# First block of a graph-attention layer: four whole products of 65 weight columns in place of tiles of columns

## The chip, the cores and the metric

The kernel runs on one NeuronCore of a Trainium2 chip. The metric is the device time of one execution in microseconds (us). TensorE (PE in the profile) multiplies, VectorE is DVE, ScalarE is ACT, GpSimd is POOL, SyncE is SP. TensorE's clock has two levels here, 1.2 GHz (granted clock 0.50) and 2.4 GHz (1.00).

## The reference, cut to what matters

A graph of 3125 nodes and 53125 edges goes through a layer norm, two graph-attention layers (four heads of 64 channels, then one of 256), a second norm and a mixture of eight experts, two per node. The change sits in the first attention layer:

```
h = (x @ W1).reshape(n, 4, 64)
es = (h * a_src).sum(-1);  ed = (h * a_dst).sum(-1)
e = leaky_relu(es[src] + ed[dst], 0.2)
w = exp(e - segment_max(e, dst)[dst])
den = segment_sum(w, dst)
out = segment_sum(h[src] * (w / den[dst])[:, :, None], dst)
```

For each destination node and head the kernel needs a sum of 64 values over its sources and one sum of weights (`den`), 65 numbers in all.

## The kernel before, in words

Nodes lie in 25 tiles of 128. `c[s, d]` counts the edges from source s to destination d. For most destinations the layer is computed densely: a matrix of weights, source by destination, is built for each head and multiplied by a table `slots` which holds, for each source and head, 64 values and one column of row factors.

Layer 1 takes its destinations in five blocks (`B1`): block 0 is one tile (128 columns), blocks 1 to 4 are three tiles (384 columns). A block has 25 **steps**, one per source tile; the step's number over all blocks is q, so block 0 is q = 0 to 24. In a step, in this order of dependence:

- ACT (L1062, four instructions, one per head) writes the ratios into one of three buffers `S1` (in `ring_a`). For buffer q it waits until TensorE has finished step q - 3.
- DVE (L1958) multiplies them by the counts in `arena`. In block 0 it then scales the table tile s + 2 (`scale`, L1848), and it builds the one-hot rows for the next step's visits (L1696, and L1700 three times).
- PE makes three **passes** (L1350). Pass 0 computes the values of heads 0 and 1 as two tiles of 64 columns of the array side by side, into the two halves of bank 0. Pass 1 does heads 2 and 3 in bank 1. Pass 2 computes the four weight sums as four tiles of 32 columns in bank 2, from one column that is repeated 32 times. So a step has eight matmuls in fp32, and each of them shows as two MATMUL records in the trace.
- Ahead of each pass PE makes one **visit** (L1198), a bf16 matmul over the whole array that counts edges for a later block: three visits, of 400, 275 and 175 columns, make one **window** of 16 destinations in one bank. ACT copies a finished window into `arena` (`window_out`, L910), after it has written `S1` of the step two later. The windows take turns in banks 3, 4 and 5 (`BANK_AT`); only the first 8 use two banks, 4 and 5.

After a block's last step ACT copies the sums to `spare` (`sums_out`, L1017), and PE must wait for each copy (semaphore `s_ot`) before it writes that bank in the next block. Then PE turns the sums so that nodes lie on partitions (L1312, L1314; "spread").

Destinations that are not in a dense block are reached edge by edge, in pairs of windows: POOL gathers their table rows (L830) once SP has stored all 25 scaled tiles (L726). Each pair is multiplied in a given step, the first in q = 28 (`PAIR1`), and its weights are made by DVE one step ahead.

The order on each engine is written out by hand as loops over q; nothing reorders it.

Of the kernel before, what the change touches and what calls it, by code (L numbers as in the profile page):

```python
# [5 lines left out]
P = 128  # L6
# [21 lines left out]
VISITS = 3  # L28
# [108 lines left out]
    USES += [("window", w) for w, v, u in VISITS_AT.get(_q, ()) if v == 0]  # L137
    USES += [("pair", p) for p in PAIR1_AT.get(_q, ())]
USE_OF = {_use: _n for _n, _use in enumerate(USES)}
N_EARLY = B1[0][1] * PER_TILE  # L140
BANK_AT = [4 + n % 2 if n < N_EARLY else 3 + n % 3 for n in range(len(USES))]
USE_BEFORE = [max((m for m in range(n) if BANK_AT[m] == BANK_AT[n]), default=None) for n in range(len(USES))]

# [104 lines left out]
def build(nc, x, src, dst, g_w1, g_a1s, g_a1d, g_b1, g_lng, g_lnb, g_w2, g_a2s, g_a2d, g_b2,  # L248
# [19 lines left out]
    with ExitStack() as ctx:  # L268
# [157 lines left out]
        vT = F2[0:NT * HEADS, 0:P]  # L426
        Wg = ring_a[:, 0:NT * P].rearrange("p (s n) -> p s n", s=NT)
        OT = spare[:, 0:PASSES * 384].rearrange("p (h n) -> p h n", h=PASSES)
        Ct = spare[:, 0:1600].bitcast(u16).rearrange("p (s n) -> p s n", s=NT)
        gd_f, glo_f, ghi_f, gkk_f = (spare[:, k * GCOLS:(k + 1) * GCOLS] for k in range(4))  # L430
        wbase = spare[:, 4 * GCOLS:4 * GCOLS + WCOLS]
# [461 lines left out]
        def _(act):  # L893
# [118 lines left out]
            def sums_out(b):  # L1012
                n = B1[b][1] * P
                after(act, s_tr, B1[b][0])
                for i in range(PASSES):
                    act.wait_ge(s_mm, ((b + 1) * NT - 1) * PASSES + i + 1)
                    act.activation(OT[:, i, 0:n], bank[i][:, 0:n], ACT.Copy).then_inc(s_ot, 1)  # L1017

# [155 lines left out]
        def _(pe):  # L1174
# [128 lines left out]
            def hooks1(q):  # L1303
                for g, i, t in tiles_at(G1, spread_of, q):
                    pe.wait_ge(s_ot, (block_of(t) + 1) * PASSES)
                    after(pe, s_TS, NT + TURNS_BEFORE["spread", t])
                    after(pe, s_xb, SPREADS_BEFORE["spread", t])
                    if t == 0:
                        pe.wait_ge(s_lk, 2)
                    by_head = bank[6][:, 0:W1T].rearrange("p (h c) -> p h c", c=CH + 1)  # L1310
                    for k in range(HEADS // 2):
                        pe.matmul(by_head[:, 2 * k:2 * k + 2, 0:CH], OT[:, k, i * P:(i + 1) * P],  # L1312
                                  ident[:, :].rearrange("p (h c) -> p h c", h=2), start=True, stop=True)
                    pe.matmul(by_head[:, :, CH], OT[:, HEADS // 2, i * P:(i + 1) * P], ident[:, 0:P:PW], start=True, stop=True).then_inc(s_tr, 1)  # L1314
                for g, i, t in tiles_at(G1, turn_of, q):
                    pe.wait_ge(s_xn, NT + E1[t] + 1)
                    pe.wait_ge(s_TS, NT + TURNS_BEFORE["turn", t])
                    after(pe, s_xb, SPREADS_BEFORE["turn", t])
                    for k in range(2):
                        ins = pe.transpose(bank[6][:, k * P:(k + 1) * P], xn[:, E1[t] % 4, k * P:(k + 1) * P], ident[:, :])  # L1320
                    ins.then_inc(s_T, 1)
                for g, i, t in tiles_at(G1, turn_of, q, 3):
                    e = E1[t]
                    pe.wait_ge(s_TS, NT + e + 1)
                    pe.wait_ge(s_HS, NT + e)
                    pe.wait_ge(s_HE, NT + e)
                    for k in range(2):
                        ins = pe.matmul(bank[7][:, 0:D + 2], xnT[:, e % 4, k, :], w2a[:, k, :], start=(k == 0), stop=(k == 1))
                    ins.then_inc(s_H, 1)

            q = 0
            for b, (t0, kt) in enumerate(B1):
                w_ = kt * P
                for s in range(NT):
# [4 lines left out]
                    for i in range(PASSES):  # L1339
# [4 lines left out]
                        if s == 0 and b:  # L1344
                            pe.wait_ge(s_ot, (b - 1) * PASSES + i + 1)
                        values = i < HEADS // 2
                        for h in range(2 * i, 2 * i + 2) if values else range(HEADS):
                            to = bank[i][h % 2 * CH:(h % 2 + 1) * CH, 0:w_] if values else bank[i][h * PW:(h + 1) * PW, 0:w_]
                            weights = row[:, h, 0:CH] if values else row[:, h, CH:CH + 1].broadcast_to([P, PW])
                            ins = pe.matmul(to, weights, S1[q % SLOTS1][:, h * w_:(h + 1) * w_], start=(s == 0), stop=(s == NT - 1))  # L1350
# [839 lines left out]
```

## Time and profile before

| | |
|---|---|
| median of 3 runs | 1428.64 us |
| the three runs | 1430.99, 1428.64, 1409.08 us |
| the profiled execution | 1437.54 us |
| span of its trace | 1435.5 us |
| mean granted clock of TensorE | 0.896 |
| TensorE matmul busy | 1216.6 us, 85% of the span |
| DVE busy | 853.8 us, 59% |
| ACT busy | 702.5 us, 49% |
| POOL busy | 711.8 us, 50% |

Busy shares are means over stages that have different limits. The slices of the page show where TensorE is busy and which clock it had; the chain of waits shows which engine sets the end; the timeline shows one step, instruction by instruction. A start in the timeline is more exact than a duration, since matmuls overlap and their ends are modelled: the price of a piece of work in a row of such pieces is read from one start to the next.

### The profile page before, as it was taken

The page shows a single profiled execution, that of the slowest core. Times are in us where ns is not written, and L with a number is a line of the kernel's source. Part 1 is how long each engine was busy: PE and PEld are TensorE (multiplying, and loading weights), DVE is VectorE, ACT ScalarE, POOL GpSimd, SP SyncE. Part 2 cuts the span into 40 slices and gives each one's busy share as a digit, 9 for nine tenths or more (in the row PEclk, how much of TensorE's full clock was granted, in tenths as well). Part 3 has the DMA queues.
Part 4 walks back from the last instruction along what each step waited for, and adds up shares of the span by engine and source line. Part 5 has one row for each costly group of instructions (what it writes and reads, how often), then busy time and mean ns, then how long its engine had stood idle before and what let it go on. Part 6 is the DMA issues. An engine that isn't in the chain of part 4 may idle for free.

```text
span 1435.5 us, 26517 instructions
## 1 busy us (share of the span) xinstructions
PE 1216.6 (85%) x8723; PEld 800.5 (56%) x8724; DVE 853.8 (59%) x2522; ACT 702.5 (49%) x1854; POOL 711.8 (50%) x621
## 2 busy tenths in 40 slices
PE   3789888888888988957787787794699999999997
PEld 3533333333333333335464565563699999999996
DVE  8677788888789979733565765786422222222221
ACT  3656566757577767833343343341434344334432
POOL 1000677676668874026665666640144445454544
PEclk9955798899999999968788899897799999999999
DMA  5232643643564382063544554544033332323221
GB/s 162 86 95 73 150 110 104 175 122 94 148 152 108 101 213 71 27 232 94 157 140 152 163 182 125 164 110 115 12 94 93 95 97 37 95 37 97 35 37 26
DMA packets 137158, 157.16 MB, mean 109 GB/s; under 512 B 58935, under 2 KB 116504, under 8 KB 137064
## 3 DMA queue, kind: packets, MB, share of 16 engines
q0 software_dynamic: 33616, 73.02, 21.5%
q1 hardware_dynamic: 102888, 82.42, 18.7%
q8 instruction: 52, 0.85, 0.2%
q10 hardware_dynamic: 560, 0.52, 0.1%
q14 instruction: 42, 0.34, 0.1%
HBM read 121.19 MB, written 35.52 MB: 109 GB/s over the span
## 4 chain that ended last, share of the span: by engine, by line
PE 50%; DVE 22%; issue 11%; ACT 5%; another core or an unknown queue 5%; DMA 4%; POOL 2%; DVEq 0%; POOLq 0%; SPq 0%; ACTq 0%
PE bank L1480 11%; PE bank L1488 11%; PE bank L1350 10%; PE bank L1431 6%; DVE ring_a L1958 4%; PE bank L1198 3%; ACT ring_a L1062 2%; DVE ohk L1700 2%; POOL arena L830 2%; DVE ring_a L2018 2%; DMA out_x<-ring_a,si 2%; PE bank L1401 1%; DVE st L1553 1%; DVE ohs L1696 1%
## 5 line engine op out<-in xcount | busy, mean ns | idle before, releaser
L830 POOL DMA_INDIRECT arena<-rows,idx_e x365 | 411.9, 1128 | 334.0 <-issue 90.6
L1350 PE MATMUL bank<-ring_a,slots 128*64 128x384 f32 (+1 forms) x2000 | 331.1, 518 | 44.6 <-DVE ring_a L1958 34.5
L1431 PE MATMUL bank<-h2t,ring_a 128*128 128x257 f32 x700 | 194.0, 423 | 29.5 <-DVE ring_a L2018 15.6
L1958 DVE SCALAR_TENSOR_TENSOR ring_a<-ring_a,arena 128x1536 f32<-128x1536 f32 (+1 forms) x125 | 192.6, 1541 | 41.9 <-ACT ring_a L1062 28.7
L1062 ACT ACTIVATE ring_a<-vbb,slots 128x384 f32<-128x384 f32 x400 | 212.2, 605 | 7.2 <-DMA vbb<-v_rows 4.1
L1170 ACT ACTIVATE ring_a<-bank,cols 128x128 f32<-128x128 f32 x432 | 129.0, 371 | 160.9 <-PE bank L1480 160.6
L1431 PEld LDWEIGHTS bank<-h2t,ring_a 128*128 128x128 f32 x700 | 141.4, 212 | 66.2 <-issue 29.1
L1350 PEld LDWEIGHTS bank<-ring_a,slots 128*64 128x64 f32 x2000 | 81.5, 136 | 133.0 <-issue 64.4
L876 POOL DMA_INDIRECT gs<-gates,gk x54 | 51.4, 951 | 149.3 <-DVE gk L2110 136.0
L1480 PEld LDWEIGHTS bank<-ring_a,arena 128*128 128x128 f32 x1056 | 123.1, 192 | 1.7
L1480 PE MATMUL bank<-ring_a,arena 128*128 128x128 f32 x1056 | 123.2, 275 | 0.0
L1488 PE MATMUL bank<-arena,ring_a 128*128 128x256 f32 x528 | 119.4, 379 | 0.0
L1198 PE MATMUL bank<-ohk,ohs 128*128 128x400 bf16 x336 | 112.1, 340 | 7.9 <-DVE ohk L1700 3.7
L830 POOL DMA_INDIRECT vbb<-rows,idx_e x75 | 98.2, 1309 | 36.1 <-issue 17.7
L2018 DVE SCALAR_TENSOR_TENSOR ring_a<-ring_a,p,arena 128x256 f32<-128x256 f32 x175 | 79.4, 480 | 58.3 <-ACT ring_a L1141 46.4
L2106 DVE TENSOR_SCALAR ring_a<-bank,cols 128x128 f32<-128x128 f32 x110 | 40.1, 406 | 118.8 <-PE bank L1463 111.8
L1141 ACT ACTIVATE ring_a<-vbb,np,pu 128x256 f32<-128x256 f32 x175 | 95.9, 590 | 28.7 <-remote 24.2
L865 POOL DMA_INDIRECT ring_a<-xtab,gi x55 | 54.3, 988 | 108.6 <-DVE gi L2098 98.3
L1488 PEld LDWEIGHTS bank<-arena,ring_a 128*128 128x128 f32 x528 | 97.7, 190 | 11.9
L870 POOL DMA_INDIRECT out_x<-ring_a,si x55 | 89.6, 1628 | 21.1 <-issue 16.3
L2114 DVE TENSOR_TENSOR ring_a<-bank,vbb 128x256 f32<-128x256 f32 x54 | 22.9, 425 | 125.3 <-PE bank L1488 119.0
L1198 PEld LDWEIGHTS bank<-ohk,ohs 128*128 128x128 bf16 x336 | 33.8, 101 | 112.0 <-issue 66.6
(308 smaller groups left out, 1709.4 us busy)
## 6 DMA issues: line engine op xcount, KB each, us to landing
counts_all<-arena SPq DMA_DIRECT2D x14, 800.0 KB
arena<-counts_all SPq DMA_DIRECT2D x14, 800.0 KB
arena<-in_L_ffn_W SPq DMA_DIRECT2D x8, 1024.0 KB, 7.4
vbb<-v_pairs SPq DMA_DIRECT2D x23, 320.0 KB
arena<-rows,idx_e POOLq DMA_INDIRECT x365
XB<-general_sums SPq DMA_DIRECT2D x38, 130.0 KB
vbb<-in_L_ffn_W SPq DMA_DIRECT2D x4, 1024.0 KB
spare<-in_L_ffn_W SPq DMA_DIRECT2D x4, 1024.0 KB
```

The costliest lines, as they stand in the source:

```text
L830: pool.indirect_dma_start(to[:, k, 0:width], None, table, bass.IndirectOffsetOnAxis(idx_e[:, m * PAIR + k:m * PAIR + k + 1], 0)).then_inc( ...
L870: pool.indirect_dma_start(out, bass.IndirectOffsetOnAxis(si[:, 0:1], 0), ys, None, bounds_check=N - 1, oob_is_err=False, compute_op=ALU.ad ...
L1062: ins = act.activation(S1[q % SLOTS1][:, h * k * P:(h + 1) * k * P].rearrange("p (t n) -> p t n", n=P), (vb1 if b else vb0)[:, 0:k, h, :], ...
L1141: act.activation(S2[m % SLOTS2][:, 0:k * P], vb2[j % 2][:, 0:k * P], ACT.Relu, scale=pu2[:, s, 0:1], bias=np2[:, s, 0:1]).then_inc(s_r, 1)
L1170: act.activation(hid[:, f, :], bank[HB[f // 2]][:, (f % 2) * P:(f % 2 + 1) * P], ACT.Gelu, bias=cols[:, ds(e * FC + f, 1)]).then_inc(s_hg, 1)
L1198: pe.matmul(bank_of(("window", w))[:, 0:KEYS].rearrange("p (h d) -> p h d", d=WIN)[:, :, lo:hi], ohs[:, w % 4, v, :], ohk[:, u % 8, 0:NT * ...
L1350: ins = pe.matmul(to, weights, S1[q % SLOTS1][:, h * w_:(h + 1) * w_], start=(s == 0), stop=(s == NT - 1))
L1431: ins = pe.matmul(bank[(j % 2) * 2 + i][:, 0:W2T], S2[q2 % SLOTS2][:, i * P:(i + 1) * P], h2t[:, s, 0:W2T], start=(s == 0), stop=(s == NT ...
L1480: ins = pe.matmul(bank[HB[f // 2]][:, (f % 2) * P:(f % 2 + 1) * P], fw1[c][:, k, f * P:(f + 1) * P], xeT[:, k, :], start=(k == 0), stop=(k ...
L1488: ins = pe.matmul(bank[3][:, 0:D], hid[:, f, :], fw2[c][:, f, :], start=(f == 0), stop=(f == FC - 1))
L1958: v.scalar_tensor_tensor(a, a, 1.0, C1[b][:, s, 0:k * P].unsqueeze(1).broadcast_to([P, HEADS, k * P]), ALU.max, ALU.mult).then_inc(s_a, 1)
L2018: v.scalar_tensor_tensor(a, a, p2[:, s, 0:1], C2[j % 2][:, 0:k, s, :], ALU.add, ALU.mult).then_inc(s_a, 1)
```

## The change

In block 0 alone PE makes, for each head, one matmul with all 65 columns of the head's table row (64 values and the factor) as weights, into partitions 0 to 64 of a bank of its own: heads 0 to 3 in banks 0 to 3. Pass 0 holds head 0, pass 1 head 1, pass 2 heads 2 and 3. Eight matmuls a step become four. Blocks 1 to 4 stay as they were.

What follows from it: bank 3 is no longer free for windows in q = 0 to 25, so `N_EARLY` grows and these windows take turns in banks 4 and 5. `sums_out(0)` copies four pieces of 65 partitions instead of three of 128. The spread of tile 0 is four transposes instead of three matmuls.

```diff
-N_EARLY = B1[0][1] * PER_TILE
+N_EARLY = N_FIRST // VISITS + len({w for q in range(NT + 1) for w, v, u in VISITS_AT.get(q, ()) if v == 0})
+assert PAIR1[0] > NT
 BANK_AT = [4 + n % 2 if n < N_EARLY else 3 + n % 3 for n in range(len(USES))]
...
+        OT0 = spare[0:CH + 1, 0:HEADS * P]
...
             def sums_out(b):
-                for i in range(PASSES):
+                for h in range(HEADS) if b == 0 else ():
+                    act.wait_ge(s_mm, (NT - 1) * PASSES + min(h + 1, PASSES))
+                    ins = act.activation(OT0[:, h * P:(h + 1) * P], bank[h][0:CH + 1, 0:P], ACT.Copy)
+                    if h != PASSES - 1:
+                        ins.then_inc(s_ot, 1)
+                for i in range(PASSES) if b else ():
...
+                    if t == 0:
+                        for h in range(HEADS):
+                            ins = pe.transpose(bank[6][:, h * (CH + 1):(h + 1) * (CH + 1)], OT0[:, h * P:(h + 1) * P], ident[0:CH + 1, 0:CH + 1])
+                        ins.then_inc(s_tr, 1)
+                        continue
...
-                        for h in range(2 * i, 2 * i + 2) if values else range(HEADS):
+                        for h in range(i, HEADS if i == PASSES - 1 else i + 1) if b == 0 else ():
+                            ins = pe.matmul(bank[h][0:CH + 1, 0:P], slots[:, s, h * (CH + 1):(h + 1) * (CH + 1)],
+                                            S1[q % SLOTS1][:, h * P:(h + 1) * P], start=(s == 0), stop=(s == NT - 1))
+                        for h in () if b == 0 else range(2 * i, 2 * i + 2) if values else range(HEADS):
```

PE in steps q = 0 and 1, before. The visits are the rows with `ohk,ohs` (25x11 is 275 columns, 25x7 is 175), the passes are those with `ring_a,slots` (weight columns x moving columns):

```order
L1198 MATMUL bank5<-ohk,ohs 128x400
L1350 MATMUL bank0<-ring_a,slots 64x128 x2
L1198 MATMUL bank5<-ohk,ohs 128x25x11
L1350 MATMUL bank1<-ring_a,slots 64x128 x2
L1198 MATMUL bank5<-ohk,ohs 128x25x7
L1350 MATMUL bank2<-ring_a,slots 32x128 x4
L1198 MATMUL bank3<-ohk,ohs 128x400
L1350 MATMUL bank0<-ring_a,slots 64x128 x2
```

The same place now:

```order
L1205 MATMUL bank4<-ohk,ohs 128x400
L1360 MATMUL bank0<-ring_a,slots 65x128
L1205 MATMUL bank4<-ohk,ohs 128x25x11
L1360 MATMUL bank1<-ring_a,slots 65x128
L1205 MATMUL bank4<-ohk,ohs 128x25x7
L1360 MATMUL bank2<-ring_a,slots 65x128
L1360 MATMUL bank3<-ring_a,slots 65x128
L1205 MATMUL bank5<-ohk,ohs 128x400
```

Every matmul of a step now takes 65 or 128 weight columns, where full-width and tiled ones alternated, and the windows no longer use bank 3.

ACT from the last window of block 0 to the copies of its sums (q = 25 and 26), before:

```order
L1062 ACTIVATE ring_a<-vbb,slots 128x384 [waits step_summed,v_rows_loaded]
L1062 ACTIVATE ring_a<-vbb,slots 128x384 x3
L910 ACTIVATE arena<-bank4 128x25x16 [waits visits_summed]
L1062 ACTIVATE ring_a<-vbb,slots 128x384 [waits step_summed]
L1062 ACTIVATE ring_a<-vbb,slots 128x384 x3
L1017 ACTIVATE spare<-bank0 128x128 [waits step_summed]
L1017 ACTIVATE spare<-bank1 128x128 [waits step_summed]
L1017 ACTIVATE spare<-bank2 128x128 [waits step_summed]
```

The same place now:

```order
L1069 ACTIVATE ring_a<-vbb,slots 128x384 [waits step_summed,v_rows_loaded]
L1069 ACTIVATE ring_a<-vbb,slots 128x384 x3
L912 ACTIVATE arena<-bank5 128x25x16 [waits visits_summed]
L1069 ACTIVATE ring_a<-vbb,slots 128x384 [waits step_summed]
L1069 ACTIVATE ring_a<-vbb,slots 128x384 x3
L1019 ACTIVATE spare<-bank0 65x128 [waits step_summed]
L1019 ACTIVATE spare<-bank1 65x128 [waits step_summed]
L1019 ACTIVATE spare<-bank2 65x128 [waits step_summed]
L1019 ACTIVATE spare<-bank3 65x128 [waits step_summed]
```

There is one copy more, at the same place.

## Rows read from the trace of the kernel before

**Rows 1.** The page: TensorE's busy tenths and clock in 40 slices.

```profile
PE   3789888888888988957787787794699999999997
...
PEclk9955798899999999968788899897799999999999
```

**Rows 2.** The chain of waits from 76 to 150 us, shares by line.

```profile
by line: PE bank L1350 61.5%; PE bank L1198 34.8%; PE bank L1207 1.7%; DVE ring_a L1958 0.9%; DVE slots L1848 0.9%; DVE arena L1954 0.3%; issue 0.2%; DVEq L1955 0.0%
```

**Rows 3.** Stretches: us, length, PE busy (last row PE, PEld, DVE, ACT, POOL), clock, DMA.

```profile
67.30:70.70 3.40, 1.04 (x6) 1.00 0.02 5
...
152.60:156.00 3.40, 3.26 (x10) 0.50 1.01 234
156.00:159.40 3.40, 2.73 (x18) 1.00 1.24 291
363.00:380.00 17.00, 16.73 (x175) 1.00 0.45 121
...
77.50:150.30 72.80, 72.76 (x482) 28.61 (x482) 53.10 (x148) 44.52 (x122) 7.12 (x7) 0.50 0.29 91
```

**Rows 4.** Timeline of TensorE in q = 1 (start us, us, engine, line, operation).

```profile
80.02 0.52 PE L1198 MATMUL bank<-ohk,ohs 128*128 128x400 bf16 x1
...
80.46 0.70 PE L1350 MATMUL bank<-ring_a,slots 128*64 128x128 f32 x4
...
81.09 0.43 PE L1198 MATMUL bank<-ohk,ohs 128*128 128x275 bf16 x1
...
81.45 0.69 PE L1350 MATMUL bank<-ring_a,slots 128*64 128x128 f32 x4
...
82.08 0.35 PE L1198 MATMUL bank<-ohk,ohs 128*128 128x175 bf16 x1
...
82.35 0.66 PE L1350 MATMUL bank<-ring_a,slots 128*32 128x128 f32 x8
...
82.94 0.52 PE L1198 MATMUL bank<-ohk,ohs 128*128 128x400 bf16 x1
```

**Rows 5.** Full-width and lone 64-column matmuls, weight loads (min/median/max ns), and clock.

```profile
70.63 2.06 PE L1267 MATMUL bank<-ident,v 128*128 128x128 f32 x8 [1.47 <-ACT v L963]
...
1060.90 1.84 PE L1480 MATMUL bank<-ring_a,arena 128*128 128x128 f32 x15
...
L1480 PEld LDWEIGHTS bank<-ring_a,arena x1056: 190/192/192, 1045.8 to 1422.3; 128*128 128x128 f32 x176
...
1009.62 12.63 PE L1454 MATMUL bank<-h2t,arena 128*64 128x128 f32 x100 [8.70 <-ACT arena L1157]
...
1009.30:1012.70 3.40, 3.08 (x15) 0.50 0.00 0
1012.70:1016.10 3.40, 3.40 (x33) 0.99 0.00 0
```

**Rows 6.** Timeline of DVE: its multiply in q = 1 and in q = 4.

```profile
78.82 0.68 DVE L1958 SCALAR_TENSOR_TENSOR ring_a<-ring_a,arena 128x512 f32<-128x512 f32 x1
...
84.88 0.68 DVE L1958 SCALAR_TENSOR_TENSOR ring_a<-ring_a,arena 128x512 f32<-128x512 f32 x1
```

**Rows 7.** Timeline of ACT in one step of block 0.

```profile
82.46 0.50 ACT L910 ACTIVATE arena<-bank 128x400 uint16<-128x400 f32 x1 [1.03 <-PE bank L1198]
83.08 1.28 ACT L1062 ACTIVATE ring_a<-vb,slots 128x128 f32<-128x128 f32 x4
```

**Rows 8.** Timeline at the end of block 0 (PE and ACT).

```profile
147.71 0.35 PE L1198 MATMUL bank<-ohk,ohs 128*128 128x175 bf16 x1
...
151.77 0.28 ACT L1017 ACTIVATE spare<-bank 128x128 f32<-128x128 f32 x1 [0.76 <-PE bank L1350]
...
152.19 1.55 PE L1350 MATMUL bank<-ring_a,slots 128*64 128x384 f32 x4 [1.46 <-ACT spare L1017]
```

**Rows 9.** POOL's first gather, and SP's stores of the 25 scaled tiles.

```profile
141.36 1.44 POOL L830 DMA_INDIRECT arena<-rows,idx_e  x1 [65.95 <-DMA rows<-slots]
...
81.81 57.88 SPq L726 DMA_DIRECT2D rows<-slots  x25
```

## The prediction

> **What bounds the kernel now.** I read the page first. TensorE is busy in nine tenths of the third and fourth slices, and these are the only two slices with a granted clock of 0.5 [rows 1]. A slice is 35.9 us, so they cover 72 to 144 us, which is block 0 of layer 1. The stretch from 77.5 to 150.3 us says the same closer up: PE is busy in 72.76 of 72.80 us, all of it at clock 0.50, that is at 1.2 GHz, while DVE is busy for 53.10 and ACT for 44.52 us [rows 3]. The chain of waits confirms it: L1350 and L1198, both PE's, hold 96% of it [rows 2]. So here TensorE sets the pace. Later in the layer that is no longer so plain, since PE runs at 2.4 GHz for most of the time and is delayed by DVE and ACT.
>
> Next, one step. From the visit of q = 1 to that of q = 2 is 82.94 - 80.02 = 2.92 us [rows 4]; 25 of these are 73 us, as the stretch has. The starts give each piece's price: visits 0.44, 0.36 and 0.27 us, passes 0.63, 0.63 and 0.59 us. A visit has 400, 275 or 175 columns, and the three prices lie on a line of (0.44 - 0.27) / 225 = 0.76 ns a column, close to one column per cycle at 1.2 GHz (0.83 ns). At 0.83 ns the columns account for 0.33, 0.23 and 0.15 us, and 0.11 to 0.13 us is left in each. This remainder appears where the array goes over from full width to tiles. The passes have a similar one: 128 columns in two records at 0.83 ns each are 0.21 + 0.21 = 0.43 us, and 0.16 to 0.20 us is left in each. Together the six remainders are 0.9 us of 2.92.
>
> What comes next if PE gets faster? DVE: its multiply of q = 1 starts at 78.82 and that of q = 4 at 84.88 us, before TensorE holds it back, so one step costs DVE 6.06 / 3 = 2.02 us [rows 6]. ACT: from the start of a window copy to the next `S1` is 83.08 - 82.46 = 0.62 us, and four `S1` instructions take 1.28 us [rows 7], 1.9 us a step. Both are close behind PE.
>
> **The change, part by part.**
>
> *Matmuls, clock unchanged.* Removed are three passes of 1.85 us. Added are four matmuls of two records each. The rows for a full-width fp32 matmul with 128 moving columns are L1267 at the low clock: eight records in 2.06 us, the last one some 0.42 long, so (2.06 - 0.42) / 7 = 0.234 us from one to the next [rows 5]. Eight are 1.87 us. The visits lose their remainder, as nothing changes width any more: 850 columns at 0.83 ns are 0.71 us. The step becomes 2.58 us; with the records at their bare columns (0.213 us) it would be 2.41 us. So the matmuls alone are no cheaper than before (1.87 against 1.85), and the gain of 0.34 to 0.51 us is in the changes of width, or 8.5 to 12.8 us over 25 steps.
>
> *The clock.* This decides the size. The clock was at 1.00 until 70.7 us, in a stretch where PE was busy for only 1.04 of 3.4 us, and then fell [rows 3]. It then stayed at 0.50 for all of block 0 although PE shows as busy without a break. It rose at 156.0 us, after a stretch with passes of 384 columns, in which the remainders weigh less [rows 3]. It rose too at 1012.7 us, after 3.4 us of L1454, which are back-to-back fp32 matmuls of only 64 weight columns by 128 moving ones [rows 5]. That is the nearest row to the new step: half of the array's columns in use, no change of width, short matmuls. So I take it that the new, gapless step raises the clock within the first few steps. At 2.4 GHz a record costs (1.84 - 0.275) / 14 = 0.112 us (L1480, fifteen records in 1.84 us, the last 0.275 long [rows 5]), the step 8 x 0.112 + 0.35 = 1.25 us, so PE would then wait for DVE in each step. Does the clock last through such short waits? In 363 to 380 us, in block 2, with the tiles' changes of width in every step, it is 1.00 throughout [rows 3]; it fell only after a stretch that was mostly idle. I take yes.
>
> *Block 0 with a fast clock* is then paced by DVE at 2.02 us, or up to 2.1 if ACT at 1.9 us gets in its way. DVE's first product was ready at 77.5 us. At the end the last window of block 0 is visited in q = 23; then come ACT's copy, the added loops, the multiply of q = 25 and its first pass. That chain took 152.19 - 147.71 = 4.5 us [rows 8], of which nothing is changed. The visit itself comes about 0.8 us after the product of q = 23 (two of the new matmuls and two visits at the fast clock). So the first pass of block 1 starts at 77.5 + 23 x 2.02 + 0.8 + 4.5 = 129.3 us instead of 152.19: 22.9 us less. With 2.1 us a step it is 21.0 less, and the two or three steps ahead of the clock's rise may cost 0.5 to 1 of it. I take 22.
>
> *The fourth copy* of sums on ACT costs one L1017, 0.28 us [rows 8], and PE waits on these copies: at most 0.3 us. At nothing I put two things. The transposes in the spread of tile 0 are eight records or fewer in the place of six. The two banks for windows: a window of step q - 2 is copied some 0.5 us after its third visit, and PE needs its bank only in step q, about 1.8 us later even at 2.02 us a step; that slack is the cover, and if it were gone each step would be longer by what the copy lacks.
>
> *Block 1's start* ran at the low clock until 156.0 us; passes of 384 columns took 1.55 us there [rows 8]. At twice the clock they would take about half of it, 0.8 us, a gain of 0 to 1.5 us, zero if DVE's multiply or a copy ends last.
>
> *Behind it.* The gathers started when the last scaled tile was stored, at 141.36 us, with the scaling spread over the steps [rows 9]. They move up with DVE, by some 20 us, as do the counts. The stores went out every 57.88 / 25 = 2.3 us because the scaling was that slow; DMA is busy for only 0.29 of that time [rows 3]. So nothing that runs by its own clock stands in the way, and the 22 us should reach the end.
>
> *The sum* against the profiled execution: 1437.5 - 22 = 1415.5 us. That execution is 8.9 us above the median of the runs shown, so the median becomes 1428.64 - 22 = 1406.6, say **1407 us**. A hint from the runs: the fastest one before, 1409.08, is 21.9 us below the slowest. That is what block 0 at the high clock would be worth, and I suspect that this run had it. No trace shows it.
>
> **The rivals.**
>
> *The clock stays low.* Then the gain is 8.5 to 12.8 us and the time 1416 to 1420 us. For it speaks that the tiles of 32 and 64 columns are busy without a break in the profile and that this raised nothing for 72 us; against it, L1454. 0.13.
>
> *More than 28.6 us,* which is 2% and about what a measurement of this kernel can tell from no change. It needs the 24 us of the upper ends and another 5 from blocks 1 to 4, whose low stretches (slices with clock 0.7 and 0.8 [rows 1]) would have to be fewer when they start with a fast clock. Below 1400 us. 0.11.
>
> *The gain is given back at the pairs.* If the stores of the tiles can't go faster than one in 2.3 us, the last ends at 139.7 us as before, the first five gathers about 8 us after it, near 149. The first pair is needed by DVE in q = 27, which would come near 137. TensorE would wait 12 us, and the time would be 1417 to 1421; with further gathers late up to 1428. Against it stands the DMA share of 0.29. 0.07.
>
> *Slower: exposed weight loads.* A full-width matmul fills the array, and if its next weights could not be loaded while it streams, each record would pay for its load. The nearest load is 0.19 us (L1480 [rows 5]): 8 x (0.234 + 0.19) + 0.71 = 4.10 us a step, 1.18 more than now, or 29.5 us: 1458 us. It decides from (2.92 - 0.71) / 8 - 0.213 = 0.063 us of exposed load per record. Against it: L1480's records follow each other every 0.112 us though each load lasts 0.19, so loads do lie beside matmuls of full width. 0.03. (The Trainium skill, page "TensorE: Matmul & The Clock Gate", section "Part 3: Packing small matmuls — row/col tiling", says that a weight load overlaps with running matmuls only where its row group differs. By that rule this rival would hold, for all these matmuls use all rows; the trace disagrees, with 0.112 against 0.19 us.)
>
> **How the numbers follow.** The forecast, a fast clock and DVE's pace, has 0.66 and 1400 to 1414 us: 20 to 24 us of gain, with some 4 us of scatter in what follows. Low clock 0.13, over 2% 0.11, given back 0.07, slower 0.03. A range of **1398 to 1420 us** leaves out most of the third case's lower part, the worst of the fourth and the fifth, less than 2 in 10. Faster by over 2% is 0.11 and a little of the forecast's edge, 0.12; slower 0.03; within 2% 0.85.
>
> **What would show it.** In the changed profile: the third and fourth slices with a clock near 1 and PE below nine tenths; block 0's steps 2.0 to 2.1 us apart with PE's idle time ended by DVE L1958's counterpart; records of 65 columns 0.11 us apart; the first 384-column pass near 130 us; the first gather near 121 us. If the steps are 2.4 to 2.6 us at clock 0.50, the step on the clock is wrong. If block 0 is short and the end hardly moves, it is the pairs. If PE is idle ahead of a 400-column visit until ACT's window copy, it is the two banks.

## The result, and the profile after

| | before | after |
|---|---|---|
| median of 20 runs each, same chip | 1430.52 us | 1412.55 us |
| lowest and highest | 1409.08, 1443.45 | 1399.39, 1428.24 |
| profiled execution, span of its trace | 1437.54, 1435.5 | 1423.93, 1421.9 |
| mean granted clock of TensorE | 0.896 | 0.916 |

The medians are 18.0 us apart. The ratio after to before is 0.9903, with a 95% interval of 0.9878 to 0.9928: faster, by less than 2%. The ratios here leave out the slowest runs of either kernel, those more than 1.5% above its fastest, so they are not the quotients of the medians of all runs.

The page of the changed kernel, TensorE's busy tenths and its clock in 40 slices of 35.5 us:

```profile
PE   3777888889889888757868787783899999999997
...
PEclk9989998879999989867989889696899999999999
```

The third and fourth slices had 8 and 9 tenths busy (the prediction says nine for both) at clock 0.5 [rows 1]; now they have 7 and 7 tenths, at 0.8 and 0.9. The chain of waits from 76 to 125 us:

```profile
by line: DVE ohk L1715 27.9%; DVE ring_a L1973 27.6%; DVE ohs L1711 21.1%; DVE slots L1863 17.5%; DMA rows<-slots 4.3%; issue 1.8%; DVE arena L1969 0.4%; DVE h2t L1983 0.1%; DVEq L1970 0.0%
```

TensorE, which held 96% of this chain [rows 2], is gone from it; DVE's lines hold almost 95%. The stretches of the changed kernel (us, length, busy time of PE, PEld, DVE, ACT and POOL with their instructions, clock, DMA share, GB/s):

```profile
77.50:81.40 3.90, 3.51 (x16) 3.14 (x17) 3.90 (x13) 1.90 (x7) 0.00 (x0) 0.50 0.20 33
81.40:100.00 18.60, 14.68 (x117) 11.59 (x115) 18.57 (x56) 16.55 (x51) 0.00 (x0) 1.00 0.52 168
100.00:125.00 25.00, 18.24 (x136) 14.17 (x137) 25.00 (x75) 21.16 (x62) 0.00 (x0) 1.00 0.22 75
125.00:129.20 4.20, 1.89 (x17) 1.54 (x15) 3.45 (x9) 4.20 (x13) 3.39 (x3) 1.00 0.87 261
129.20:136.00 6.80, 6.39 (x23) 1.40 (x23) 6.64 (x12) 3.66 (x8) 5.58 (x5) 0.50 1.11 253
```

The clock is low for the first 4 us of block 0 only, where all 73 us were low before [rows 3]. It then stays at 1.00 although PE waits for more than a fifth of the time, and falls after 4 us in which PE had little to do, at the start of block 1. The timeline of TensorE in block 0, at the low clock, at the high one, and where it meets DVE's pace:

```profile
80.07 0.54 PE L1205 MATMUL bank<-ohk,ohs 128*128 128x400 bf16 x1
80.41 0.63 PE L1360 MATMUL bank<-ring_a,slots 128*65 128x128 f32 x2
80.83 0.46 PE L1205 MATMUL bank<-ohk,ohs 128*128 128x275 bf16 x1
81.08 0.53 PE L1360 MATMUL bank<-ring_a,slots 128*65 128x128 f32 x2
...
81.98 0.33 PE L1205 MATMUL bank<-ohk,ohs 128*128 128x400 bf16 x1
...
83.25 0.33 PE L1205 MATMUL bank<-ohk,ohs 128*128 128x400 bf16 x1
83.95 0.43 PE L1360 MATMUL bank<-ring_a,slots 128*65 128x128 f32 x2 [0.37 <-DVE ring_a L1973]
...
85.97 0.43 PE L1360 MATMUL bank<-ring_a,slots 128*65 128x128 f32 x2 [0.54 <-DVE ring_a L1973]
```

At the low clock the visit of 400 columns takes 80.41 - 80.07 = 0.34 us instead of 0.44 [rows 4]: its remainder is gone. A pass of two records takes 80.83 - 80.41 = 0.42, so a record is at the prediction's lower bound, 0.21 us, and a step would be 0.71 + 8 x 0.21 = 2.4 us. At the high clock a step is 83.25 - 81.98 = 1.27 us. Two steps later PE's first pass comes 85.97 - 83.95 = 2.02 us after the last, released by DVE. The end of block 0 (DVE, POOL, ACT, PE):

```profile
127.80 1.76 DVE L1973 SCALAR_TENSOR_TENSOR ring_a<-ring_a,arena 128x1536 f32<-128x1536 f32 x1
...
125.19 1.22 POOL L832 DMA_INDIRECT arena<-rows,idx_e  x1 [49.85 <-DMA rows<-slots]
...
128.38 0.74 ACT L1019 ACTIVATE spare<-bank 65x128 f32<-65x128 f32 x4
...
129.61 1.55 PE L1365 MATMUL bank<-ring_a,slots 128*64 128x384 f32 x4 [2.71 <-DVE ring_a L1973]
```

Block 1's first pass stands at 129.61 instead of 152.19 us, 22.6 less [rows 8]; the first gather at 125.19 instead of 141.36, 16.2 less [rows 9]. What the lead becomes is read by DVE's multiplies (L1973, before L1958), one a step, in one trace of each kernel on this chip and one of each on the chip of set 1 below:

| start us of | before | after | second chip, before | second chip, after |
|---|---|---|---|---|
| multiply of q = 0 | 76.8 | 77.1 | 77.7 | 77.1 |
| q = 25 | 149.9 | 127.8 | 150.9 | 127.7 |
| q = 29 | 169.9 | 144.5 | 165.1 | 144.5 |
| q = 50 | 270.4 | 245.9 | 255.7 | 237.5 |
| q = 124, the last | 609.2 | 585.3 | 581.8 | 563.9 |
| end of the span | 1435.5 | 1421.9 | 1364.9 | 1347.3 |

The lead is 22.1 and 23.2 us at q = 25, 23.9 and 17.9 at the end of layer 1, and 13.6 and 17.6 at the end of the span. (The profiled execution of the changed kernel is one of its slower ones, 11.4 us above its median; that of the kernel before is 7.0 above its own.)

### The profile page after: what moved, and what is told of

Same layout as the page of the kernel before. It is cut to its first block, busy times and chain, and to the rows that moved or that the text cites. A ratio compares the mean times of both kernels' runs of the same rounds, so it can differ in the third digit from the quotient of the medians.

```text
span 1421.9 us, 26113 instructions
## 1 busy us (share of the span) xinstructions
PE 1181.7 (83%) x8521; PEld 802.2 (56%) x8522; DVE 850.6 (60%) x2522; ACT 699.0 (49%) x1855; POOL 717.6 (50%) x621
## 3 DMA queue, kind: packets, MB, share of 16 engines
q0 software_dynamic: 33616, 73.02, 21.7%
## 4 chain that ended last, share of the span: by engine, by line
PE 45%; DVE 22%; issue 12%; POOL 6%; DMA 5%; another core or an unknown queue 5%; ACT 4%; POOLq 0%; DVEq 0%; ACTq 0%
PE bank L1495 11%; PE bank L1503 11%; PE bank L1365 7%; PE bank L1446 5%; POOL arena L832 5%; DVE ring_a L1973 4%; DMA out_x<-ring_a,si 3%; DVE ohk L1715 2%; ACT ring_a L1069 2%; DVE ohs L1711 2%; PE bank L1416 2%; PE bank L1205 2%; DVE st L1568 1%; DVE ring_a L2033 1%
## 5 line engine op out<-in xcount | busy, mean ns | idle before, releaser
L832 POOL DMA_INDIRECT arena<-rows,idx_e x365 | 417.4, 1143 | 313.3 <-issue 93.6
L1365 PE MATMUL bank<-ring_a,slots 128*64 128x384 f32 (+1 forms) x1600 | 279.8, 537 | 46.4 <-DVE ring_a L1973 28.3
L1973 DVE SCALAR_TENSOR_TENSOR ring_a<-ring_a,arena 128x1536 f32<-128x1536 f32 (+1 forms) x125 | 192.3, 1539 | 27.0 <-ACT ring_a L1069 21.6
L1365 PEld LDWEIGHTS bank<-ring_a,slots 128*64 128x64 f32 (+1 forms) x1600 | 61.7, 127 | 115.8 <-issue 54.3
L1205 PE MATMUL bank<-ohk,ohs 128*128 128x400 bf16 x336 | 102.9, 312 | 8.4 <-DVE ohk L1715 3.7
L1205 PEld LDWEIGHTS bank<-ohk,ohs 128*128 128x128 bf16 x336 | 33.5, 100 | 88.2 <-issue 57.2
```

The costliest lines, as they stand in the source:

```text
L832: pool.indirect_dma_start(to[:, k, 0:width], None, table, bass.IndirectOffsetOnAxis(idx_e[:, m * PAIR + k:m * PAIR + k + 1], 0)).then_inc( ...
L1205: pe.matmul(bank_of(("window", w))[:, 0:KEYS].rearrange("p (h d) -> p h d", d=WIN)[:, :, lo:hi], ohs[:, w % 4, v, :], ohk[:, u % 8, 0:NT * ...
L1973: v.scalar_tensor_tensor(a, a, 1.0, C1[b][:, s, 0:k * P].unsqueeze(1).broadcast_to([P, HEADS, k * P]), ALU.max, ALU.mult).then_inc(s_a, 1)
```

## The experiments

Theory A: the gain is the clock. With changes of width between short matmuls TensorE pauses in each step, its clock stays low, and PE's 2.92 us pace block 0; at the high clock DVE's 2.02 us do, in whatever form the products are made. Rival B: the gain is in the matmuls themselves, cheaper without tiles at any clock. Rival C, for the part of the 22 us that is missing at the end: the pairs of block 1, which came nearer to their gathers.

The kernels ran in three sets, each on one chip with the kernel before beside it. "Low" is the time at clock 0.50 between the multiplies of q = 0 and q = 24.

| kernel | median us (runs) | ratio to before, 95% | q = 0 to 24, us | low, us |
|---|---|---|---|---|
| set 1: before | 1364.73 (25) | | | |
| before_again | 1366.34 (4) | 1.0106 [1.0007, 1.0205] | 67.4 | 67.4 |
| after_again | 1347.22 (10) | 0.9921 [0.9883, 0.9959] | 47.2 | 4.8 |
| warm_tiles | 1348.66 (10) | 0.9945 [0.9906, 0.9984] | 47.2 | 0.3 |
| grouped_visits | 1350.49 (10) | 0.9958 [0.9919, 0.9997] | 47.2 | 7.1 |
| set 2: before | 1433.25 (13) | | | |
| two_banks | 1431.38 (10) | 1.0054 [1.0000, 1.0107] | 67.4 | 67.4 |
| after_filled | 1412.91 (4) | 0.9831 [0.9781, 0.9881] | 47.2 | 4.2 |
| late_pairs | 1408.72 (4) | 0.9796 [0.9747, 0.9844] | 47.2 | 4.0 |
| pool_scale | 1414.47 (4) | 0.9850 [0.9796, 0.9903] | 57.2 | 31.1 |
| set 3: before | 1428.36 (29) | | | |
| mid_fill | 1423.00 (10) | 1.0001 [0.9963, 1.0038] | 60.0 | 38.2 |
| before_late | 1436.80 (10) | 0.9977 [0.9912, 1.0043] | 67.4 | 67.4 |
| after_third | 1413.27 (12) | 0.9919 [0.9877, 0.9961] | 47.2 | 3.8 |
| late_pairs_again | 1404.13 (6) | 0.9790 [0.9721, 0.9858] | 47.2 | 4.8 |

### The two kernels again, on another chip

**before_again**, unchanged:

> The kernel before, unchanged, for a second trace. Theory A (the changed kernel's block 0 gains about 23 us, from the clock and DVE's pace, and the 9 us that the profiled pair lost again in layer 2, 344.8 against 336.8 us from its first to its last multiply, is scatter between executions): block 0 again at clock 0.50 with steps of 2.9 us, and layer 2 in this trace anywhere between 334 and 346 us. Rival (the shorter layer 1 makes layer 2 longer, since what shifts is met by transfers in another way): layer 2 here again within 2 us of 336.8. Ratio 1.00 in both.

It shows how far a ratio here can be trusted: 1.0106 for the same kernel, with an interval whose lower end just clears 1. The executions of this kernel differ in the clock that they were granted, which is taken up again with the prediction's hint below.

**after_again**, the changed kernel:

> The changed kernel, unchanged, for a second trace. Theory A: block 0's steps at 2.02 us, first pass of block 1 near 129.6 us, layer 2 anywhere between 334 and 346 us, ratio to before 0.985 to 0.992. Rival (layer 2 gives time back): layer 2 again within 2 us of 344.8.

The medians are 17.5 us apart, as on the first chip. The time as a whole is some 65 us lower on this chip for both, in layer 2 above all: 292.3 and 293.0 us from its first to its last multiply, 336.8 and 344.8 on the first chip. Both expectations for layer 2 missed these values; since the two kernels differ by 0.7 us here, a shorter layer 1 does not by itself lengthen layer 2.

### Is it the clock, or the form of the products?

**warm_tiles** is the kernel before, with all its tiles of columns, and three full-width matmuls ahead of PE's loop, while PE has nothing to do:

```diff
+            for _ in range(3):
+                pe.matmul(bank[2][:, :], ones[:, :], w1a[:, :, :].rearrange("p k n -> p (k n)")[:, 0:512], start=True, stop=True)
             q = 0
```

> The kernel before, tiles of columns and all, with three extra full-width fp32 matmuls of 512 columns (their result is never read) placed on TensorE just ahead of block 0, where it waits. They take about 5.1 us at the low clock, 2 us more than the wait, and should raise the clock before the first step. Theory A (the gain of the change is the clock; tiles at the high clock need less than DVE's 2.02 us a step): steps of 2.0 to 2.1 us at clock 1.00 all through block 0, 18 to 21 us faster than before, ratio 0.985 to 0.988, so as fast as the changed kernel. Rival B (the tiled form cannot hold the high clock, or is itself the price): the clock falls back within a few steps, block 0 takes over 68 us, ratio above 0.996.

**grouped_visits** is the kernel before with a step's three visits ahead of its first pass in block 0, so that it changes width twice in a step and not six times:

```diff
-                        if work:
+                        while work and (b == 0 or len(work) == PER_STEP - i):
                             visit(*work.pop(0))
```

> The kernel before with one thing changed: in block 0 the three visits of a step stand together ahead of the three passes, which stay tiles of columns. The array changes between full width and tiles twice a step, not six times. Theory A (the pauses at these changes are what kept the clock low): low-clock steps of 2.93 - 4 x 0.12 = 2.45 us at most for the first few, then clock 1.00 and steps of 2.0 to 2.1 us; block 0 in 50 to 54 us, ratio 0.984 to 0.990. Rival B (tiles of columns themselves keep the clock low, whatever stands between them): clock 0.50 throughout, steps of 2.45 us, block 0 in 61 us, ratio 0.991 to 0.993.

Stretches of warm_tiles, of grouped_visits and of before_again, columns as above:

```profile
77.50:81.00 3.50, 3.50 (x39) 1.58 (x37) 3.50 (x12) 1.89 (x6) 0.00 (x0) 1.00 0.33 80
81.00:84.50 3.50, 3.36 (x34) 1.52 (x30) 3.50 (x12) 3.10 (x10) 0.00 (x0) 1.00 0.73 194
84.50:125.00 40.50, 37.96 (x391) 17.45 (x390) 40.47 (x121) 33.86 (x101) 0.78 (x1) 1.00 0.32 112
```

```profile
77.50:81.00 3.50, 3.50 (x31) 1.87 (x35) 3.50 (x12) 1.89 (x6) 0.00 (x0) 0.50 0.33 93
81.00:84.50 3.50, 3.50 (x32) 1.67 (x34) 3.50 (x11) 2.16 (x7) 0.00 (x0) 0.62 0.74 259
84.50:125.00 40.50, 32.71 (x408) 18.17 (x408) 40.47 (x121) 34.67 (x105) 0.76 (x1) 1.00 0.30 105
```

```profile
84.50:125.00 40.50, 40.50 (x266) 16.05 (x266) 30.26 (x85) 24.45 (x70) 0.00 (x0) 0.50 0.23 82
```

The same tiles hold 1.00 for all of block 0 once the clock was high ahead of them, and 0.50 when it was not; at 1.00 DVE is full in 40.47 of 40.50 us and the 24 steps take 47.2 us, as with whole products. Grouping lifts the clock too, within some 6 us of the first pass. So in steps that start at the low clock it is how often the width changes that keeps them at 0.50; what about the changes the clock answers to is not shown, for the profile has PE busy throughout in before_again too. By the medians both kernels gain 14 to 16 of the 17.5 us. Their ratios, 0.9945 and 0.9958, missed the 0.984 to 0.990 that I expected, and their intervals overlap with that of after_again. Rival B falls as the account of this gain: with the old products and a high clock block 0 is as short, because a step of either form then takes TensorE less than DVE's 2.02 us (1.27 us whole, 1.81 tiled, see mid_fill). At the low clock whole products would still be shorter, 2.4 against 2.92 us by the estimate above; no run holds them there with TensorE setting the pace.

**mid_fill** puts the same three matmuls (into bank 7) in the middle of block 0 of the kernel before:

```diff
+                        if q == 12 and i == 0:
+                            for _ in range(3):
+                                pe.matmul(bank[7][:, :], ...)
                         if i == 0:
                             pe.wait_ge(s_a, q + 1)
```

> The kernel before, with three full-width fp32 matmuls of 512 columns put into PE's queue in q = 12 of block 0, ahead of that step's first pass; their result is not used. Clock theory (both clocks hold themselves in tiled steps: a full-width stretch lifts the clock, and nothing in the tiled steps lowers it): q = 0 to 11 run at clock 0.50 with steps of 2.9 us, q = 13 to 24 at 1.00 with steps of 2.0 us. The three matmuls cost 3 to 5 us, so the multiply of q = 25 comes 12 x 0.9 - 4 = about 7 us sooner than in the kernel before, and the execution is about 0.4% shorter. Rival, an effect of how the layer starts (only a clock that is high at the first visit lasts): the clock falls back within a few steps of q = 12, and the kernel is 3 to 5 us slower.

Timeline of TensorE in mid_fill ahead of q = 12 and behind it:

```profile
107.54 0.52 PE L1198 MATMUL bank<-ohk,ohs 128*128 128x400 bf16 x1
...
110.47 0.52 PE L1198 MATMUL bank<-ohk,ohs 128*128 128x400 bf16 x1
...
113.70 2.48 PE L1344 MATMUL bank<-w1a,ones 128*128 128x512 f32 x4
...
118.51 0.34 PE L1198 MATMUL bank<-ohk,ohs 128*128 128x400 bf16 x1
118.78 0.44 PE L1353 MATMUL bank<-ring_a,slots 128*64 128x128 f32 x4
...
120.32 0.34 PE L1198 MATMUL bank<-ohk,ohs 128*128 128x400 bf16 x1
```

Steps of 2.93 us become steps of 1.81 us, which are tiled steps at the high clock without a gap, and they stay so: the stretch from 116 to 125 us has 9.00 us of PE at 1.00. So both states hold themselves in the same code. The multiply of q = 25 comes at 140.6 us, 9.3 earlier than before; 7 was expected, since I had taken DVE's 2.02 us for a PE that was behind and catching up. The rival, that only a clock that is high at the first visit lasts, falls. In the time little of it is seen: the medians are 5.4 us apart, and the ratio shows nothing. (Eight of the 29 executions of before in this set, 1405.9 to 1423.8 us, had a mean granted clock of 0.914 to 0.925, about as high as the ten of mid_fill with 0.910 to 0.922; the other 21 had 0.896 to 0.908.)

**two_banks** has only the change's `N_EARLY` line, which takes bank 3 from the windows:

> The kernel before with one piece of the change alone: the windows of q = 0 to 25 take turns in banks 4 and 5 and leave bank 3 out. Theory A (the two banks cost nothing, since a window is copied long before its bank comes round again): steps of 2.93 us at clock 0.50, no wait of TensorE for a window copy, ratio 1.00, as the kernel before. Rival B (TensorE waits for copies): steps longer by 0.1 us or more, or waits that end with ACT's copy, 2.5 us or more slower.

The block takes as long as before, and no wait for a bank is in its trace. At nothing, as costed.

**pool_scale** is the changed kernel with the 25 scalings on POOL, ahead of block 0, to take them out of DVE's step:

```diff
+            pool.wait_ge(s_vt, 1)
+            pool.wait_ge(s_ex, 2)
+            for t in range(NT):
+                ...
+                pool.tensor_tensor(row, row, p1[:, t, :].unsqueeze(2).broadcast_to([P, HEADS, CH + 1]), ALU.mult).then_inc(s_scl, 1)
...
-            scale(0)
-            scale(1)
...
-                    if b == 0 and s + 2 < NT:
-                        scale(s + 2)
```

> The changed kernel with the 25 scalings of the table moved from DVE to POOL, which has nothing to do during block 0; POOL's clearing of the weight columns follows them. Theory A (block 0 is now paced by DVE's sum of 2.02 us a step): DVE's step loses 0.34 us and falls to 1.68, so that ACT's 1.9 us sets the pace; block 0 shorter by 2 to 3 us; the table is stored earlier, the gathers start some 20 us earlier and the wait of 2.6 us for them is gone; together 4 to 6 us faster than the changed kernel. Rival B (POOL's scalings lie beside DVE's work and slow it down, or are themselves slower than 2 us each): steps stay at 2.0 us or grow, at most the 2.6 us of the gathers are gained.

Stretches of pool_scale, and DVE while POOL scales:

```profile
84.50:95.00 10.50, 8.28 (x35) 6.51 (x36) 10.50 (x21) 4.83 (x15) 8.24 (x11) 0.50 1.07 341
95.00:105.00 10.00, 9.92 (x76) 8.38 (x74) 8.86 (x27) 8.71 (x28) 3.46 (x3) 0.88 0.46 157
...
115.00:120.00 5.00, 2.62 (x11) 2.01 (x11) 2.02 (x6) 1.76 (x6) 3.79 (x4) 0.50 0.42 108
```

```profile
83.62 1.14 DVE L1976 SCALAR_TENSOR_TENSOR ring_a<-ring_a,arena 128x512 f32<-128x512 f32 x1
84.69 0.97 DVE L1716 TENSOR_TENSOR ohs<-iota_b,lo_s 128x384 bf16<-128x384 bf16 x1
...
87.29 1.14 DVE L1976 SCALAR_TENSOR_TENSOR ring_a<-ring_a,arena 128x512 f32<-128x512 f32 x1
```

While POOL computes, DVE's multiply lasts 1.14 us instead of 0.68 and its step 3.67 instead of 2.02. TensorE waits for it, and the clock stays low although the products are the whole ones. So whole products alone don't lift it; it rose only when PE had no pauses left, and fell again near 115 us, where TensorE waited 2.9 us ahead of a visit. Block 0 ends 10 us later than in the changed kernel, about half of it by q = 12; 4 to 6 us of gain had been expected. The gathers start 24 us earlier, at 100.7 us, and the time is much the same.

### Where the rest of the gain went

**after_filled** keeps the clock up at the start of block 1, by three such matmuls into bank 7 ahead of its first pass (`if b == 1 and s == 0 and i == 0`):

> The changed kernel with three extra full-width fp32 matmuls of 512 columns (result never read) where TensorE waits at the start of block 1, between its first visit and its first pass; they take 2.6 us at the high clock, about the wait of 2.7 us. In the changed kernel the clock falls there for 6.8 us and passes of 384 columns take 1.55 us. Theory A (this low stretch costs block 1 something): clock 1.00 through q = 25 to 27, first three passes of block 1 0.9 us each, 1 to 2.5 us faster than the changed kernel. Rival B (DVE and the gathers end last there anyway): clock high, but a gain under 0.5 us.

The clock stays at 1.00 from 124 to 140 us, and the multiply of q = 28 comes 62.3 us after that of q = 0, in the changed kernel 62.2: nothing is gained there, because DVE waits for gathers, in every trace with the change:

```profile
124.03 0.43 PE L1363 MATMUL bank<-ring_a,slots 128*65 128x128 f32 x2 [0.54 <-DVE ring_a L1976]
...
129.10 0.87 PE L1368 MATMUL bank<-ring_a,slots 128*64 128x384 f32 x4
...
134.85 0.48 DVE L1878 TENSOR_TENSOR hit<-place,dst_e 128x320 f32<-128x320 f32 x1
136.97 0.49 DVE L1897 TENSOR_TENSOR ring_a<-arena,vbb 128x320 f32<-128x320 f32 x1 [1.65 <-DMA arena<-rows,idx_e]
137.50 0.49 DVE L1901 SCALAR_TENSOR_TENSOR ring_a<-ring_a,hit 128x320 f32<-128x320 f32 x1
...
142.07 0.49 DVE L1897 TENSOR_TENSOR ring_a<-arena,vbb 128x320 f32<-128x320 f32 x1 [0.94 <-DMA arena<-rows,idx_e]
```

**late_pairs**, and again in another set as **late_pairs_again**, is the changed kernel with the pairs over q = 32 to 112 instead of 28 to 112:

```diff
-PAIR1 = [28 + p * 86 // PAIRS for p in range(PAIRS)]
+PAIR1 = [32 + p * 82 // PAIRS for p in range(PAIRS)]
```

> The changed kernel with the pairs of windows started four steps later: the first in q = 32, the last in q = 112 as before. In the two traces of the other chip the lead of the changed kernel shrank from 23.15 to 20.6 us at q = 28 and 29, where DVE waited 2.6 us for the first gathers. Theory A (those 2.6 us are the price of a shorter block 0, because the gathers start only 2.8 us ahead of block 1 and not 8.6): no wait for gathers in block 1, the lead still near 23 us at q = 30, 2 to 3 us faster than the changed kernel, 19 to 21 us faster than before by the medians. Rival B (the steps are then denser later, and other waits take the room, as PE, DVE and ACT are all near their limits there): lead 23 us at q = 30 but 18 us or less at q = 124, no faster than the changed kernel.

> The changed kernel with its pairs spread over q = 32 to 112. If the waits of q = 28 and 29 are given back, it is 1.5 to 2.6 us shorter than the changed kernel on the same chip at the end of layer 1 and in the time (ratio 0.1 to 0.2% lower). Rival: the later pairs meet late gathers too and nothing is left of it.

**after_third** is the changed kernel beside it:

> The changed kernel, for the comparison with late_pairs_again on the same chip: block 0 in 50.6 us, first pass of block 1 near 129.6 us, waits of 2 to 3 us in q = 28 and 29, and 16 to 22 us less than the kernel before.

**before_late** is the same line in the kernel before:

> The kernel before, with its pairs spread over q = 32 to 112 in place of 28 to 112; nothing else changed. If late pairs help only because the changed kernel's first gathers come too close to their use, nothing is gained here: layer 1 ends within 1 us of the kernel before, since its gathers have 8.6 us of lead over block 1. Rival: moving pairs out of block 1 helps any version, by the 2 us that late_pairs stood ahead of after_filled at the end of layer 1.

With late pairs the multiply of q = 28 comes 59.8 and 59.5 us after that of q = 0, and 62.2 to 62.5 in the four traces with the change and the pairs as they were, 2.4 to 3.0 us more. This is not the price of the waits alone: ahead of q = 28 DVE waits 1.5 to 1.8 us and spends another 1.4 on the pair's own instructions (the three rows above), which late pairs only move. The waits ahead of q = 28 and 29 together are 2.5 to 2.6 us in each of the four traces. From the first multiply of layer 1 to the last it is 506.0 and 504.0 us against 508.1, 508.0 and 510.8 in the traces of the changed kernel and after_filled on such chips. (In between the lead over these changes from step to step, up to 19 us at q = 61, since the moved pairs take their work along.) In set 3 the medians are 9.1 us apart and the two intervals don't touch, far more than the 0.1 to 0.2% expected; in set 2 late_pairs is 4.2 us below after_filled, with intervals that overlap. In the kernel before the same line brings nothing: a ratio of 0.9977 with a median 8.4 us above that of before, which also shows how far medians of this set wander. Its layer 1 takes 537.1 us, against 532.4 in the trace of before and 530.7 in that of two_banks, where at most 1 us of difference was expected: before_late waits 11.7 us for gathers in the layer, the kernel before 4.5.

On the second chip there are more waits for gathers later in the layer. What DVE waited for ahead of its product with gathered rows in all of layer 1, in after_again (L1894) and in before_again (L1879):

```profile
its engine sat idle before it (us, times) until:
  DMA arena<-rows,idx_e: 11.2, 5
  DMA vbb<-rows,idx_e: 1.3, 2
```

```profile
its engine sat idle before it (us, times) until:
  DMA arena<-rows,idx_e: 4.3, 1
  DMA vbb<-rows,idx_e: 0.9, 1
```

That is 12.5 us against 5.2, 7.3 more, in the pair of traces where the lead falls by 23.2 - 17.9 = 5.3 us. The other two traces of this chip with a short block 0 say the same: warm_tiles and grouped_visits wait 3.3 us for the first pairs, 9.1 and 11.2 in the layer, and their leads fall from q = 25 to q = 29 by 3.3 and 3.4 us, that of after_again, with its 2.6 us of waits, by 2.6. On the first chip the waits are 6.5 us, 1.5 of them ahead of q = 28 and marked "issue", against 4.5, and there the lead holds to the end of the layer. So rival C is shown for the first pairs: the waits are there in all six traces with a block 0 of 47.2 us and the pairs as they were, and on the second chip the lead falls by as much. That the later waits on that chip come from the shorter block 0 too is likely, but no run separates it. What late pairs bring is less clear: the waits ahead of q = 28 and 29 are gone both times, but in the whole layer one of its traces waits 9.5 us for gathers and the other not at all. That the time gains more than 2.6 us rests on set 3, and no trace settles where it comes from. The best medians are those of the change with late pairs, 1404 and 1409 us, in set 2 not clear of after_filled.

## Why the prediction was nearly right

The time, 1412.55 us, lies in the range and in the forecast case of 1400 to 1414 us. The gain, 18.0 us, is less than the 20 to 24 of that case. Of the 5.9 us between the forecast's 1406.6 and the time, 1.9 are the median of before, which rose from 1428.64 to 1430.52 with more runs, and 4.0 are missing gain. The mechanism in block 0 came as forecast; what follows takes it term by term.

**The clock** rose, as the nearest row said (L1454, [rows 5]). It was the step of the argument that decided the size, and it is shown from both sides: old products at a high clock make block 0 as short (warm_tiles), new products with pauses don't lift it (pool_scale). That it would last through short waits also held, for 44 us with PE idle a quarter of the time. My reason, half of the columns in use and no change of width, named more than it needed: grouped_visits lifts it with tiles.

**Pace of block 0**: 2.02 us from DVE was forecast and 2.02 found. The first pass of block 1 was put at 129.3 us and came at 129.61.

**Cost of the matmuls.** A step at the high clock was put at 1.25 us and took 1.27. At the low clock the lower end, 0.213 us a record, was right, not the 0.234 that I took. Its working was wrong all the same: 128 columns at 0.83 ns are 0.11 us, not 0.21. An fp32 record takes twice as long per column as a bf16 visit: 0.21 us for 128 columns are 1.6 ns a column at the low clock, where the visits have about 0.8, and the six records of 512 columns ahead of block 0 in warm_tiles take 4.91 us, 0.82 each, at a clock of 0.55. The sum of the step used the right 0.21, so nothing else changes by it.

**Weight loads.** In the changed kernel twelve records of L1360 take 1.48 us from 125.24 us on, the last some 0.275 of it, so one every (1.48 - 0.275) / 11 = 0.110 us, while twelve loads fill 1.32 us beside them:

```profile
125.16 1.32 PEld L1360 LDWEIGHTS bank<-ring_a,slots 128*65 128x65 f32 x12
125.24 1.48 PE L1360 MATMUL bank<-ring_a,slots 128*65 128x128 f32 x12
```

They lie beside the matmuls, and this rival fell. (The Trainium skill, page "TensorE: Matmul & The Clock Gate", section "Part 3: Packing small matmuls — row/col tiling", lets a load overlap only where its row group differs; these all use every row, and the trace disagrees again.)

**The fourth copy, the two banks.** Four copies of 65 partitions take 0.74 us and end at 129.12, half a microsecond ahead of the first pass, which waits for DVE. Both cost nothing.

**Block 1's start** was given 0 to 1.5 us. It was zero: the clock fell again at 129.2 us, and after_filled shows that with a high clock the pairs take it back.

**The first gather** came at 125.19 us, not at 121. I had moved it with DVE's whole lead. But it hangs on the last scaling, in q = 22, whose multiply came 138.3 - 121.8 = 16.5 us sooner, as much as the gather. Most of the rest of the lead arises behind it: TensorE took up the product of q = 22 4.2 us after it was ready (139.0 to 143.2 us), and now at once (122.47 to 122.52). So the gathers' lead over the first multiply of block 1 shrank from 149.9 - 141.4 = 8.5 us to 127.8 - 125.2 = 2.6.

**"Behind it", the step that failed.** It said that nothing stands in the way and that the 22 us reach the end. 18.0 us did, and 17.5 and 15.1 in sets 1 and 3, by the medians. Part of the rival "given back at the pairs" belonged into the sum. I had it as a case of its own at 12 us, with slow stores as its cause; the stores kept up, and the gathers were late all the same, by 2.6 us at the first pairs. On the second chip the lead fell by 5.3 us in layer 1, nearly all that was lost in its traces, with 7.3 us more of waits for gathers. On the first chip the loss in the traces lies elsewhere: layer 2 took 344.8 us against 336.8. The other traces from sets 2 and 3 have 329 to 338 us there, with the change and without, so these 8 us look like scatter, though no run isolates them.

**The hint** that the fastest run of before had a high clock in block 0 is still shown by no trace, though much speaks for it. Both states hold themselves in its steps (mid_fill). In set 1 its runs spread over 26 us, 1346.59 to 1372.73. The five fastest, up to 1354.4 us, had a mean granted clock of 0.928 to 0.938; the 14 slowest, from 1364.6 us on, had 0.910 to 0.914, and the trace of before_again, with block 0 at 0.50 throughout, has 0.911. Some 67 us of 1365 at 1.00 in place of 0.50 would add 0.025 to it (an estimate). The 30 runs of the three kernels that raise the clock lie at 1344.0 to 1352.0 us with 0.931 to 0.946. If this is so, the medians of before already hold a part of the gain: the changed kernel is 21.7 us below the median of those 14 runs, and 17.5 below that of all. It does not explain set 3, where the same comparison, with the 21 runs at 0.896 to 0.908, gives 15.7 us in place of 15.1. How much of the missing 4 us is this, how much the waits for gathers and how much scatter stays open.

## What to carry to other kernels

Where TensorE is busy without a break and yet at clock 0.50, first ask whether a stretch of full-width matmuls in a gap ahead of it lifts the clock. Here three matmuls did what a rewrite of the products did, and the time of the block was then set by the next engine, whose pace could be read beforehand. When a stretch gets shorter, compare the slack of each thing that is started in it and needed behind it: the gathers had 8.5 us and were left with 2.6, and the waits for them took about a tenth of what block 0 had gained.

## What the runs showed of the hardware

- The same 24 steps of TensorE ran at clock 0.50 throughout (67.4 us) or at 1.00 almost throughout (47.2 us), by what ran ahead of them. The tiled step took 2.92 us at the one and 1.81 at the other.
- The high clock outlasts waits of 0.4 to 0.5 us in each step of 2 us; it fell behind 4.2 us with 1.89 us of matmuls.
- An fp32 record of 128 columns takes 0.21 us at the low clock and 0.11 at the high one; records of 65 weight columns follow each other every 0.110 us beside weight loads of 0.14.
- While POOL multiplied tiles, DVE's 128x512 fp32 product went from 0.68 to 1.14 us and its 128x384 bf16 comparison from 0.55 to 0.97.
- Two chips differ by 65 us of 1430 in the same kernel, some 44 to 52 of them in layer 2.
